# The last stage's hidden rows: VectorE squares straight from PSUM, GpSimd makes the low parts

## What is computed

```python
def relu2(x):
    r = jnp.maximum(x, 0.0)
    return r * r
...
lat = xf @ fc1_w.T
xs = lat[tok]
out = jnp.zeros_like(xs)
for e in range(E):
    he = relu2(xs @ w1[e].T) @ w2[e].T
    out = jnp.where((sorted_eid == e)[:, None], he, out)
out = out * scores_sorted[:, None]
comb = jnp.zeros((N, LATENT), out.dtype).at[tok].add(out)
routed = comb @ fc2_w.T * SCALE
shared = relu2(xf @ up_w.T) @ down_w.T
return (routed + shared).reshape(Bv, Sv, D)
```

## Time and profile before

| what | value |
|---|---|
| runs | 2200.09, 2203.21, 2206.48 us; median 2203.21 us |
| profiled execution | span from first to last instruction 2200.8 us (its time around the span isn't listed separately) |
| mean granted TensorE clock | 0.944 of full speed |
| busy share of the span | PE 88%, PEld 77%, DVE 71%, ACT 43%, POOL 32% |
| stage C | from about 0.90 ms to the end; batches repeat every 171 to 175 us |

### The profile page before, as it was taken

One profiled execution on the slowest core, in us unless ns is written; L12 is line 12 of the kernel. 1 busy time (PEld: TensorE's weight loads), 2 busy tenths in 40 slices (PEclk: granted clock), 3 DMA queues, 4 the chain that ended last, 5 costly groups with the idle time before them and its releaser, 6 DMA issues.

```text
span 2200.8 us, 36370 instructions
## 1 busy us (share of the span) xinstructions
PE 1934.4 (88%) x11720; PEld 1685.3 (77%) x11752; DVE 1558.0 (71%) x3448; ACT 945.8 (43%) x1708; POOL 698.7 (32%) x611
## 2 busy tenths in 40 slices
PE   7999998279999939899899899989989989988997
PEld 6888787169999938778778788877867867977975
DVE  4788887334444535886886886886886787797687
ACT  3344353233333414454455445445445355444444
POOL 4145555500000032342342342343243244144033
PEclk8999999579999969999999999999999999999999
DMA  3422321032232231111111112111121112111011
GB/s 124 168 94 94 120 81 51 24 115 87 87 130 78 86 98 36 54 43 57 57 39 58 60 40 55 32 71 44 36 75 43 39 39 79 30 49 49 11 39 58
DMA packets 92638, 144.75 MB, mean 66 GB/s; under 512 B 14542, under 2 KB 72742, under 8 KB 91568
## 3 DMA queue, kind: packets, MB, share of 16 engines
q1 hardware_dynamic: 79120, 110.99, 15.0%
q0 software_dynamic: 13344, 31.64, 5.4%
HBM read 103.21 MB, written 48.79 MB: 69 GB/s over the span
## 4 chain that ended last, share of the span: by engine, by line
PE 31%; DVE 19%; issue 8%; ACT 3%; POOL 2%; DVEq 1%; DMA 0%; ACTq 0%; POOLq 0%
PE c_ps L118 8%; PE c_ps L119 8%; PE c_ps L120 8%; DVE c_place L1609 4%; DVE c_tmp L97 2%; PE c_ps L1684 2%; DVE c_shared_place L1604 2%; PE c_ps L127 1%; DVE c_key L97 1%; DVE c_pre L1465 1%; PE c_ps L128 1%; PE c_ps L129 1%; POOL c_shared_place L1299 1%; DVE c_place L1536 1%; DVE c_pre L1463 1%
## 5 line engine op out<-in xcount | busy, mean ns | idle before, releaser
L1609 DVE TENSOR_TENSOR c_place<-c_shared_place,c_place 128x512 fp32r<-128x512 f32 x256 | 231.5, 929 | 47.4 <-ACT c_place L1419 27.5
L118 PE MATMUL c_ps<-c_place 128*128 128x256 f32 (+1 forms) x768 | 250.5, 326 | 6.1 <-DVE c_place L1536 6.1
L120 PE MATMUL c_ps<-c_place 128*128 128x256 f32 (+1 forms) x768 | 245.1, 319 | 0.0
L119 PE MATMUL c_ps<-c_place 128*128 128x256 f32 (+1 forms) x768 | 244.6, 318 | 0.0
L1274 POOL DMA_INDIRECT c_gathered<-expert_results,c_slots x112 | 113.1, 1010 | 403.0 <-DVE c_pre L1465 382.8
L1411 ACT ACTIVATE c_shared_place<-c_ps 128x512 f32<-128x512 f32 x256 | 150.7, 596 | 195.8 <-DVE c_shared_place L1604 120.0
L1299 POOL TENSOR_TENSOR c_shared_place<-c_shared_place,c_x2T 128x512 f32<-128x512 f32 x128 | 178.1, 1399 | 172.8 <-ACT c_shared_place L1411 161.9
L1295 POOL TENSOR_TENSOR c_shared_place<-c_shared_place 128x512 f32<-128x512 f32 x128 | 140.7, 1106 | 271.6 <-ACT c_shared_place L1411 271.6
L127 PE MATMUL c_ps<-c_downT_hi,c_place 128*128 128x256 f32 x512 | 156.5, 306 | 53.4 <-DVE c_place L1609 53.4
L118 PEld LDWEIGHTS c_ps<-c_place 128*128 128x128 f32 x768 | 146.1, 190 | 18.3 <-DVE c_place L1536 7.9
L120 PEld LDWEIGHTS c_ps<-c_place 128*128 128x128 f32 x768 | 146.0, 190 | 10.7
(11 more groups left out here) (346 smaller groups left out, 5762.1 us busy)
## 6 DMA issues: line engine op xcount, KB each, us to landing
c_x2T<-score_rows SPq DMA_DIRECT2D x64, 512.0 KB, 5.4
a_xT_raw<-xT SPq DMA_DIRECT2D x8, 1024.0 KB, 6.5
a_x_rows<-x SPq DMA_DIRECT2D x8, 1024.0 KB, 5.2
x_rows<-a_x SPq DMA_DIRECT2D x8, 1024.0 KB, 4.6
c_pre<-x_rows SPq DMA_DIRECT2D x8, 1024.0 KB, 5.4
out<-c_x SPq DMA_DIRECT2D x16, 512.0 KB, 3.0
expert_rows<-a_zeros POOLq DMA_DIRECT2D x7, 1024.0 KB, 15.1
b_win_raw<-w_in SPq DMA_DIRECT2D x7, 1024.0 KB, 8.0
```

The costliest lines, as they stand in the source:

```text
L118: pe.matmul(out, lh, rh, start=(j == 0), stop=False)
L119: pe.matmul(out, lh, rl, start=False, stop=False)
L120: last = pe.matmul(out, ll, rh, start=False, stop=(j == len(terms) - 1))
L1609: v.tensor_tensor(hid_lo[:, place, :], square[:, place % RING, :], f32(hid_hi[:, place, :]), ALU.subtract).then_inc(hid_split, 1)
```

## The change

VectorE no longer makes low parts of the hidden chunks. It makes the squares, straight from PSUM, with one instruction that rectifies and multiplies: `max(psum, 0) * factor`. For a shared chunk the factor is the rectified chunk in `relu`, for an expert chunk it is the weighed chunk that GpSimd left in `square`. GpSimd makes all low parts; its squares of the shared chunks are gone. It now walks its own loop, in which the low part of an expert chunk comes two chunks (`LAG`) behind the weighing.

The bank of a chunk is freed (`s_free`) by VectorE's square and no more by ScalarE's rectifying. ScalarE waits, before it overwrites a slot of `relu`, for the square of the chunk two before.

```diff
+            def weigh(b, h, e):
+                n, place = hidden(b, "expert", (h, e // CHUNKS), e % CHUNKS)
+                pool.wait_ge(relu_done, n + 1)
+                wait_past(pool, hid_split, n - RING + 1)
+                pool.wait_ge(scores_in[e // 2], 16 * (HALVES * b + h + 1))
+                pool.tensor_tensor(square[:, place % RING, :], relu[:, place % RELU_RING, :], score_rows[:, bass.ts(e, HALF)], ALU.mult).then_inc(scaled, 1)
+            def split(b, kind, j, k):
+                n, place = hidden(b, kind, j, k)
+                pool.wait_ge(s_free, s_upto(b, (kind, j), k))
+                pool.wait_ge(hid_hi_done, n + 1)
+                pool.tensor_tensor(hid_lo[:, place, :], square[:, place % RING, :], f32(hid_hi[:, place, :]), ALU.subtract).then_inc(hid_split, 1)
...
-                        if kind == "up":
-                            pool.tensor_tensor(square[:, place % RING, :], t, t, ALU.mult).then_inc(squared, 1)
...
+                for h in range(HALVES):
+                    for part in range(PARTS):
+                        for k in range(CHUNKS):
+                            split(b, "up", (h, part), k)
+                    for e in range(EXPERTS + LAG):
+                        if e < EXPERTS:
+                            weigh(b, h, e)
+                        if e >= LAG:
+                            split(b, "expert", (h, (e - LAG) // CHUNKS), (e - LAG) % CHUNKS)
...
-                                wait_past(act, squared, n - RELU_RING + 1)
-                                if kind == "up" or k < RELU_RING:
-                                    wait_past(act, hid_hi_done, n - RELU_RING + 1)
-                                act.activation(relu[:, place % RELU_RING, :], ps[:, s_bank(unit, k), :], ACT.Relu).then_inc(s_free, 1)
+                                if place >= RELU_RING:
+                                    act.wait_ge(s_free, s_upto(b, *chunk_of(j[0], place - RELU_RING)))
+                                    if place < EXPERTS + RELU_RING:
+                                        act.wait_ge(hid_hi_done, n - RELU_RING + 1)
...
+                                act.activation(relu[:, place % RELU_RING, :], ps[:, s_bank(unit, k), :], ACT.Relu).then_inc(relu_done, 1)
...
-                                v.tensor_tensor(square[:, place % RING, :], square[:, place % RING, :], relu[:, place % RELU_RING, :], ALU.mult).then_inc(squared, 1)
...
-                                v.tensor_tensor(hid_lo[:, place, :], square[:, place % RING, :], f32(hid_hi[:, place, :]), ALU.subtract).then_inc(hid_split, 1)
...
+                            v.scalar_tensor_tensor(square[:, place % RING, :], ps[:, s_bank(unit, k), :], 0.0, factor, ALU.max, ALU.mult).then_inc(s_free, 1)
```

42 lines of the change are left out of this document (17 added, 25 removed).

## The result

The changed kernel takes 2217.4 us (median of 10 runs, 2213.2 to 2222.0); the kernel before took 2203.9 us beside it (10 runs). The ratio is 1.0054, 95% interval 1.0037 to 1.0071. It is slower, by 13.5 us at the medians, where the prediction said 34 to 35. The profiled execution has a span of 2214.5 us, against 2200.8.

A forecast was written before the change was run, and what follows sets the result against it. Stage C was taken as bound by TensorE, with VectorE's order setting its start on the shared result. 8 x 4.4 = 35 us on the 2200.8 us span gives 2236, plus 2.4: 2238 us, range 2187 to 2275.

The forecast's parts named there:

- the chains are held: ln2 and ln4: small VectorE instructions get one through per GpSimd instruction; ln2 ends at 1441.1 instead of 1438.81.
- the chains aren't held: Faster rival: several small VectorE instructions slip between two of GpSimd's in ln2 and ln4; 2187 us, chance 0.14.
- the pace of GpSimd: GpSimd's low parts and weighings in the hidden chunks: taken as 1.25 us each.
- rival of 1.04 us: Same-time rival: a GpSimd low part is as cheap as its square; 2203 to 2211 us, chance 0.14.
- the one of 1.40 us: Slower rival: GpSimd's instructions stretch beside VectorE, holding from 1.35 us on; 2269 us, chance 0.2.
- the bubble: Expert chunks: GpSimd's weighing of chunk 12 waits about 0.85 us for square, high part and rectifying behind chunk 11's weighing.
- the first bank: Before up (0,1): TensorE stands still from 1418.9 to 1422.2, until VectorE's first square frees a bank.
- sum for TensorE: 0: Shared chunks, first half: a 5.8 us wait traded for waits of 3.3, 1.6 and 2.4 us, net zero.
- 1.8 us late: Routing behind chunk 15's high part, end of first half: done at 1469.05 against 1467.24.
- run of 14: End of each half: six weighings and eight low parts in a row on GpSimd, 17.5 us plus 0.85 us.
- one batch times eight: Only the fourth batch was walked through; its 4.4 us were multiplied by eight, giving 35 us.
- the clock: Outside the sum: a TensorE wait of 2.4 to 3.4 us may or may not bring a few us at 1.2 GHz.

The follow-up runs named there:

- unread copies: Against the kernel with all low parts on VectorE, GpSimd also makes the shared chunks' low parts a second time, into cells nobody reads; ratio 1.0233.
- expert part: Changed kernel with its shared chunks put back as before (GpSimd squares, VectorE makes low parts), so only the expert chunks are changed; ratio 1.018.
- shared part: Changed kernel with its expert chunks put back as before (VectorE multiplies and makes low parts), so only the shared chunks are changed; ratio 0.9937.
- chains moved: Changed kernel with two units moved in VectorE's order: ln2 ahead of up (0,1), ln4 ahead of latent 1; ratio 1.0042.

## Why the prediction was right in direction and wrong in size

**Right: the chains are held.** Time line of VectorE in the changed kernel, fourth batch, first half, then GpSimd's at the same time:

```profile
1440.54 0.19 DVE L142 TENSOR_TENSOR c_tmp<-c_pre_stats 128x8 f32<-128x8 f32 x1
1440.65 1.32 DVE L143 TENSOR_TENSOR c_pre_shift<-c_pre_stats 128x8 f32<-128x8 f32 x1
1441.89 1.30 DVE L144 SCALAR_TENSOR_TENSOR c_tmp<-c_pre_stats 128x8 f32<-128x8 f32 x1
1443.23 1.21 DVE L97 SCALAR_TENSOR_TENSOR c_tmp<-c_tmp 128x8 f32<-128x8 f32 x1
1444.47 1.21 DVE L97 TENSOR_TENSOR c_tmp<-c_tmp 128x8 f32<-128x8 f32 x1
1445.71 0.17 DVE L97 TENSOR_SCALAR c_tmp<-c_tmp 128x8 int32<-128x8 int32 x1
```

```profile
1438.14 5.02 POOL L1296 TENSOR_TENSOR c_place<-c_shared_place,c_place 128x512 fp32r<-128x512 f32 x4 [2.02 <-DVE c_shared_place L1626]
1443.11 2.55 POOL L1289 TENSOR_TENSOR c_shared_place<-c_shared_place,c_x2T 128x512 f32<-128x512 f32 x2
1450.49 1.29 POOL L1289 TENSOR_TENSOR c_shared_place<-c_shared_place,c_x2T 128x512 f32<-128x512 f32 x1 [4.84 <-ACT c_shared_place L1430]
```

Four small instructions take 1.21 to 1.32 us each, one for each of GpSimd's. At 1445.66 GpSimd's second weighing ends, and from then on VectorE's take 0.17. The chain is 7.2 us long instead of 2.9, so the rival "the chains aren't held" falls. The prediction had five instructions held in ln2, and four are. The Trainium skill, "SBUF — State Buffer", section "SBUF: two separate sides", says that the port pair is locked for a whole instruction; these rows agree, with one instruction through at each end of GpSimd's, and so do the 1189 ns beside the unread copies.

**Right: the pace of GpSimd.** Its instructions are 1.25 us apart:

```profile
1461.22 1.29 POOL L1289 TENSOR_TENSOR c_shared_place<-c_shared_place,c_x2T 128x512 f32<-128x512 f32 x1
1462.47 1.27 POOL L1296 TENSOR_TENSOR c_place<-c_shared_place,c_place 128x512 fp32r<-128x512 f32 x1
```

The means 1304 and 1291 ns include the overlap. The rival of 1.04 us and the one of 1.40 us both fall. From the third weighing to the end of the last low part it took 18.2 us in both halves, where the prediction had 17.5 + 0.85; the bubble measured 0.71:

```profile
1456.23 1.29 POOL L1289 TENSOR_TENSOR c_shared_place<-c_shared_place,c_x2T 128x512 f32<-128x512 f32 x1 [0.71 <-ACT c_shared_place L1430]
```

**Right: the first bank.** The wait for it was put at 3.3 us, and is 3.3 at the longest, eight times. ScalarE shows the same hold:

```profile
1430.42 0.60 ACT L1430 ACTIVATE c_shared_place<-c_ps 128x512 f32<-128x512 f32 x1 [4.90 <-DVE c_shared_place L1626]
```

**Wrong: the shared chunks, "sum for TensorE: 0", and the routing, "1.8 us late".** These are the terms that failed. Here is the walk of the fourth batch, in us from its first rectifying (1414.85 before, 1423.04 after):

| step | before | predicted | measured |
|---|---|---|---|
| first square | | +6.55 | +6.6 |
| first square of up (0,1), behind the two combines | | +15.25 | +14.3 |
| last shared low part, half 0 | +21.15 | +21.35 | +20.1 |
| third weighing | | +29.0 | +27.45 |
| last low part, half 0 | +42.95 | +47.35 | +45.65 |
| routing of half 1 done | +52.4 | +54.2 | +52.0 |
| last shared low part, half 1 | +65.9 | +67.3 | +65.5 |
| last low part, half 1 | +87.6 | +91.95 | +89.8 |

The sum of 0 was wrong as it stood: 3.3, 1.6 and 2.4 are 7.3 us, traded for 5.8. In the run TensorE had only two long waits there:

```profile
1430.39 0.78 PE L118 MATMUL c_ps<-c_x3T_hi,c_upT_hi 128*128 128x512 f32 x1 [3.20 <-DVE c_shared_place L1626]
...
1443.22 0.39 PE L127 MATMUL c_ps<-c_downT_hi,c_place 128*128 128x256 f32 x1 [1.58 <-POOL c_place L1296]
```

The 2.4 us wait didn't come, and 4.8 us took the place of 5.8. The two combines ended 0.9 us earlier than I had them, and the shared low parts 1.2 us. Small errors of the same sign followed: 0.3 us in ln2 and what stands behind it, 0.2 in the run of 14, 0.3 in the routing itself. The routing then starts at +43.45, not +45.3, and is done 0.4 us earlier than before, not 1.8 us later. In the kernel before, it stood beside GpSimd's squares of up (1,0), which held four of its instructions (the last is L1524 with 1.07 us in the earlier trace rows), and TensorE waited for it. In the changed kernel GpSimd has nothing to do until VectorE has squared, so only two at its start are held. The transpose that needs the routing, before and after, then the end of the routing in the changed kernel:

```profile
1467.38 0.28 PE L1712 MATMUL c_ps<-c_ident,c_score_et 128*32 128x128 f32 x1 [2.08 <-DVE c_score_et L1524]
```

```profile
1476.20 0.27 PE L1729 MATMUL c_ps<-c_ident,c_score_et 128*32 128x128 f32 x1
```

```profile
1474.84 0.22 DVE L1543 TENSOR_TENSOR c_score_et<-c_score,c_row_s 128x32 f32<-128x32 f32 x1
```

The 16.2 us for the routing stood in the prediction's first paragraph, but no step of the walk says how much of them is left. So the last shared low part of half 1 comes 0.4 us earlier than before, where I had 1.4 us later. In all, the walk is 2.2 us too long, half of its 4.4 us. The run of 14 itself was sized well: 18.2 us against 18.35. The two parts alone say the same in the mean of six batches: +4.05 us for the expert part, and -2.1 us for the shared part, where I had zero.

**Wrong: one batch times eight.** The fourth batch is one of three of the loop's six in which the kernel before goes well. Its hidden parts are 87.6, 87.5 and 87.6 us in the second to fourth batches, then 89.8, 90.2 and 89.9. Here are the stretches of the kernel before with out 0, latent 1 and up (1,1), of the fourth batch and of the fifth (window, length, busy times of PE, PEld, DVE, ACT and POOL, granted clock, DMA share, GB/s):

```profile
1468.00:1482.00 14.00, 12.61 (x69) 10.62 (x71) 12.06 (x19) 7.13 (x13) 7.19 (x6) 1.00 0.42 152
...
1639.00:1655.00 16.00, 14.24 (x67) 11.65 (x69) 12.55 (x19) 7.13 (x13) 6.90 (x6) 0.89 0.39 134
```

In the fifth nearly the same work (67 and 69 matmuls) takes 2 us longer, at a granted clock of 0.89. TensorE's wait for the routing ahead of it was 2.95 us there, and 2.08 in the fourth batch. The changed kernel has 89.1 to 89.8 us in all six. So the kernel before had up to 2.7 us to lose in three of them, and lost it without the change. Against the three good batches the change costs 1.9 us a batch, against all six 0.7. One batch times eight was a choice that I should have tested on the other seven; their times stood in the same trace. The kernel before has one such trace, so whether it always loses three batches isn't shown.

Together: of the 35 us that were forecast, the walk's error takes 8 x 2.2, about 17, and the other batches about 8, which leaves the 10.0 us of the hidden parts. The rests add 7.7 and the earlier end of the code ahead takes 4.0. So 13.7 us came out partly by luck: two errors against each other, since the prediction had the hidden parts too dear and the rests at nothing.

**Left out: the clock.** The rest of a batch holds no edit, and is 1.2 us longer. The stretch of 12 us behind the last low part of half 1, in the kernel before and then in the changed one (fourth batch each):

```profile
1502.40:1514.40 12.00, 9.59 (x55) 8.15 (x55) 7.28 (x15) 4.62 (x8) 8.08 (x5) 1.00 0.37 109
```

```profile
1512.80:1524.80 12.00, 10.50 (x53) 8.97 (x54) 7.18 (x13) 4.68 (x8) 7.03 (x5) 0.88 0.15 45
```

The granted clock there, read in the same way in all six batches, and the rest that follows:

| kernel | clock in those 12 us | rest, us |
|---|---|---|
| before | 1.00 1.00 1.00 0.86 1.00 0.89 | 83.2 83.1 83.6 84.8 83.3 81.9 |
| changed | 0.79 0.83 0.88 0.83 0.88 0.87 | 86.0 85.4 83.8 85.5 84.2 82.0 |
| chains moved | 1.00 1.00 1.00 1.00 1.00 1.00 | 83.3 83.6 83.2 83.5 83.4 80.5 |
| all low parts to VectorE | 0.86 0.86 0.86 0.86 1.00 1.00 | 84.9 85.5 85.2 85.3 83.7 80.5 |

The sixth rest is shorter in all of them, since the last batch follows it. Elsewhere 1.00 goes with 83.1 to 83.7 us, and anything below with 83.8 to 86.0. 12 us at 0.86 are 1.7 us at full speed lost, about the difference. TensorE's idle time in the six rests is the same in both kernels, 20.6 us; its busy time for the same matmuls is 7.0 us longer (length, then busy times, before and after):

```profile
sum 499.85, PE 479.24 PEld 427.18 DVE 348.67 ACT 218.90 POOL 107.65; mean PE 79.87 PEld 71.20 DVE 58.11 ACT 36.48 POOL 17.94
```

```profile
sum 506.83, PE 486.20 PEld 432.63 DVE 348.58 ACT 219.57 POOL 107.44; mean PE 81.03 PEld 72.10 DVE 58.10 ACT 36.59 POOL 17.91
```

The hidden parts show it too. In the six batches TensorE is idle 1.2 us a batch less than before and busy 1.9 us more. The waits of the first table thus don't tell the price by themselves; how much of the 1.9 us is the clock isn't shown.

Before the clock fell in the changed kernel, TensorE had been stopping in `comb` for up to 1.5 us at a time for low parts. But the kernel with all low parts on VectorE hardly waits there and shows 0.86 in four batches, and the one with moved chains shows 1.00 in all six. What sets it I leave open. In the prediction the clock stood outside the sum with "may or may not"; the whole change measured 13.5 us, and 7.7 us of the spans' difference lie in these rests.

**Bounds of this account.** The experiments show the gain of the squares, the price of GpSimd's low parts, and the held chains as a cost that moving doesn't take away. Read from traces, but isolated by no run, is that the routing makes most of the 1.3 us by which the two parts together cost less than their sum. The errors of the walk are read from one batch. What sets the clock is open.

## What to carry to other kernels

Before you move work to an idle engine, look where it lands in that engine's list. Here GpSimd had been idle 68% of the time, and low parts on it cost 8 us a batch: 7.3 for those of the expert chunks, which stand between the weighings that the others wait for, and 0.7 for those of the shared chunks, beside which VectorE squares from PSUM. Work of GpSimd on SBUF operands beside VectorE's on SBUF can be dear by itself, 12 us for the unread copies. Let VectorE read one operand from PSUM where it can, since such an instruction wasn't held in any of these runs. When a change has two parts, cost and test each by itself, and walk through more than one repetition of a loop before multiplying.

## What the runs showed of the hardware beyond expectation

- Both engines pay. Beside each other VectorE's subtraction of 128x512 went from 834 to 1189 ns on average and GpSimd's from 1304 to 1519 ns. The forecast had priced only VectorE's loss; GpSimd's stood among the rivals.
- Chains of tiny instructions suffer most for their work: 16 instructions of 0.17 us, 2.97 us in all, took 7.2 us, since one got through for each GpSimd instruction of 1.25 us.
- The instruction with one operand in PSUM took 679 to 690 ns on average in every kernel, beside GpSimd or not.
- A lower granted clock for a few us behind a loop's last waits went with 1 to 2 us more a batch, where the hidden part of the changed kernel lost 0.7, and it appeared in the kernel before too, in two batches of six.
